# Two cross-attention layers written as one straight program, with the last slot of layer 1 joined to the first of layer 2

## What is computed

```python
res = x
h = _layer_norm(x, ln1_scale, ln1_offset)
x = res + _cross_attention(h, xf_1, wq1, bq1, wk1, bk1, wv1, bv1, wo1, bo1, bias_k1, bias_v1)
res = x
h = _layer_norm(x, ln2_scale, ln2_offset)
x = res + _cross_attention(h, xf_2, wq2, bq2, wk2, bk2, wv2, bv2, wo2, bo2, bias_k2, bias_v2)
```

## Time and profile before

| | |
|---|---|
| time, median of 3 runs | 1511.86 us (1509.45 to 1514.3) |
| profiled execution, first to last instruction (span) | 1511.0 us |
| mean granted PE clock | 0.966 of full speed |
| first slot starts | 34.39 us |
| layer 2 starts (its front-only slot) | 547.49 us |
| first matmul behind the two layers | 1063.45 us |

### The profile page before, as it was taken

The page is one execution under the profiler, slowest core; times in us unless marked ns, Lnnn a source line. Parts: engine busy times, 40 slices in busy tenths (PEclk is TensorE's granted clock), DMA queues, the critical chain, the costliest instruction groups (busy, mean ns, idle before and its releaser), DMA issues. The chain is left out here.

```text
span 1511.0 us, 29462 instructions
## 1 busy us (share of the span) xinstructions
PE 1426.2 (94%) x11575; PEld 1274.8 (84%) x11575; DVE 895.5 (59%) x1929; ACT 626.1 (41%) x1053; POOL 340.7 (23%) x322
## 2 busy tenths in 40 slices
PE   4999999999999899999999999998898999997898
PEld 3899899899998778988998999986787888887787
DVE  6566567566666646666665666665523377776422
ACT  4533344334333543433343344343422336666521
POOL 4201101101011111101101011020754035555654
PEclk8999999999999979999999999997899999999899
DMA  5000000000000000000000000000000000001000
GB/s 169 29 29 1 30 5 25 30 1 29 29 2 29 1 30 1 29 29 1 29 1 30 29 1 29 29 1 1 25 0 8 0 1 1 0 0 60 4 28 28
DMA packets 28991, 30.42 MB, mean 20 GB/s; under 512 B 651, under 2 KB 28883, under 8 KB 28883
## 3 DMA queue, kind: packets, MB, share of 16 engines
q1 hardware_dynamic: 28658, 28.72, 6.0%
q10 hardware_dynamic: 226, 0.10, 0.0%
HBM read 26.72 MB, written 2.10 MB: 19 GB/s over the span
## 5 line engine op out<-in xcount | busy, mean ns | idle before, releaser
L296 POOL TENSOR_TENSOR WLO<-W,WHI 128x512 fp32r<-128x512 f32 x68 | 85.1, 1283 | 793.5 <-DVE WHI L623 793.5
L168 PE MATMUL bank<-SRC_HI,WHI 128*128 128x512 f32 (+1 forms) x576 | 233.4, 405 | 18.5 <-issue 14.6
L169 PE MATMUL bank<-SRC_LO,WHI 128*128 128x512 f32 (+1 forms) x576 | 231.9, 403 | 0.0
L170 PE MATMUL bank<-SRC_HI,WLO 128*128 128x512 f32 (+1 forms) x576 | 231.5, 402 | 0.0
L570 DVE STREAM_TRANSPOSE PRT<-PR 32x256 f32<-32x256 f32 x512 | 223.3, 436 | 8.4
L591 DVE TENSOR_TENSOR CLO<-bank,CHI 128x512 fp32r<-128x512 f32 x128 | 88.2, 691 | 159.3 <-ACT CHI L502 159.1
L478 ACT ACTIVATE QT<-bank,PB 128x512 f32<-128x512 f32 x128 | 88.2, 690 | 209.2 <-PE bank L170 209.2
L168 PE MATMUL bank<-WHI,CHI 128*128 128x256 f32 x512 | 155.2, 303 | 0.0
L168 PE MATMUL bank<-WHI,SRC_HI 128*128 128x256 f32 x512 | 149.4, 292 | 0.0
L168 PEld LDWEIGHTS bank<-SRC_HI,WHI 128*128 128x128 f32 x576 | 111.2, 193 | 42.7 <-issue 15.4
L170 PE MATMUL bank<-WHI,CLO 128*128 128x256 f32 x512 | 145.6, 284 | 0.0
(11 more groups left out here) (182 smaller groups left out, 2976.5 us busy)
## 6 DMA issues: line engine op xcount, KB each, us to landing
W<-in_wall SPq DMA_DIRECT2D x18, 1024.0 KB, 5.6
V<-in_ctx SPq DMA_DIRECT2D x4, 512.0 KB, 5.5
X<-in_x SPq DMA_DIRECT2D x4, 512.0 KB, 6.5
mlp_w<-in_w SPq DMA_DIRECT2D x2, 1024.0 KB, 7.4
out<-X SPq DMA_DIRECT2D x4, 512.0 KB, 3.0
W<-in_qw SPq DMA_DIRECT2D x1, 256.0 KB, 3.9
W<-in_kw SPq DMA_DIRECT2D x1, 256.0 KB, 4.1
W<-in_vw SPq DMA_DIRECT2D x1, 256.0 KB, 4.9
```

The source lines that it names most:

```text
L168: e.matmul(dst, a_hi, b_hi, start=start, stop=False, **kw)
L169: e.matmul(dst, a_hi, b_lo, start=False, stop=False, **kw)
L170: return e.matmul(dst, a_lo, b_hi, start=False, stop=stop, **kw)
L296: i = e.tensor_tensor(WLO[a][:, j, :, :], W[a][:, j, :, :], WHI[a][:, j, :, :].bitcast(F32), ALU.subtract)
```

## The change

The hardware loops are gone: each engine's program is written out for 65 slots, numbered n = 0 to 64 over both layers. A new class works out what a slot has to do. Slot 32 has the back of layer 1's last unit and the front of layer 2's first. The norm's group 3 moves from the slot that was `at` 0 to the slot behind it: n = 1 for layer 1, n = 33 for layer 2. Waits and addresses become constants. In the bridge slots the PE program is otherwise as before.

```diff
+            class Slot:
+                def __init__(self, n):
+                    self.n, self.front, self.back = n, n < NL * UNITS, n > 0
+                    self.L, self.pair, self.g = n // UNITS, n // G, n % G
+                    self.a, self.ab = self.pair % 2, (n - 1) // G % 2
+                    self.Lb, self.hp, self.gb = (n - 1) // UNITS, (n - 1) // G % HP, (n - 1) % G
+                    self.bridge = self.back and self.hp == HP - 1
+                    self.nk, self.ng = (n + 2) // UNITS, (n + 2) % UNITS
+                    self.norm = self.back and self.ng < G
+                    self.parts = self.Lb * G + self.gb + 1
+            def slots(e, slot, begin=None):
+                for n in range(NL * UNITS + 1):
+                    if begin is not None and n % UNITS == 0 and n < NL * UNITS:
+                        begin(e, n // UNITS)
+                    slot(Slot(n))
...
 # SP
-                    with e.Fori(1, SETS // 2) as i:
-                        for a in range(2):
+                    for m in range(2, SETS):
...
 # POOL
-                    with e.Fori(0, NL) as L:
+                    for L in range(NL):
                         norm_lo(e, norm, L, G - 1)
-                        split(L * HP + 1, 1)
-                        with e.Fori(0, HP // 2 - 1) as i:
-                            for a in range(2):
-                                split(L * HP + i * 2 + 2 + a, a)
-                        split(L * HP + HP, 0)
+                        for m in range(L * HP + 1, L * HP + HP + 1):
+                            split(m, m % 2)
...
 # PE: before the key projection
-                                if j == 1 and norm_now is not None:
-                                    e.wait_ge(norm.scaled, (norm_now[0] * G + norm_now[1]) * DC)
-                                if j == 1 and at == 1:
-                                    e.wait_ge(norm.scaled, (L + 1) * G * DC)
+                                if j == 1:
+                                    if n == 0:
+                                        e.wait_ge(norm.scaled, (G - 1) * DC)
+                                    elif before.norm:
+                                        e.wait_ge(norm.scaled, (before.nk * G + before.ng + 1) * DC)
...
-                        if at == 0:
-                            e.wait_ge(k_out, 2 * n + 2)
-                            norm_turn(e, norm, *norm_now, PROJ[2:])
...
-                        if norm_now is not None and bridge and front:
-                            e.wait_ge(ptb_out, L * G + at - LASTP)
-                            norm_turn(e, norm, *norm_now, PROJ[2:])
+                        if s.norm and front:
+                            if s.bridge:
+                                e.wait_ge(ptb_out, s.parts)
+                                e.wait_ge(bw_out, s.Lb + 1)
+                            norm_turn(e, norm, s.nk, s.ng, PROJ[2:])
...
 # PE and ACT
-                    with e.Fori(0, NL) as L:
-                        slots(e, L, slot)
+                    slots(e, slot)
...
 # DVE
-                    with e.Fori(0, NL) as L:
+                    def begin(e, L):
                         e.memset(BWT[:, :, :], 0.0).then_inc(bwt_sum, 1)
                         e.wait_ge(bwt_sum, L * BWTN + 1)
-                        e.tensor_copy(BWT[:, :, H + 1], PM[:, bass.ds(L * LNP + 4, 2)]).then_inc(bwt_sum, 1)
-                        slots(e, L, slot)
+                        e.tensor_copy(BWT[:, :, H + 1], PM[:, L * LNP + 4:L * LNP + 6]).then_inc(bwt_sum, 1)
+                    slots(e, slot, begin)
```

More of the change, by code:

```diff
@@ L317, in _, with slot @@
                 def _(e):
[L318 to L320 removed]
+                    def slot(s):
+                        n, g, a, front, back = s.n, s.g, s.a, s.front, s.back
                         toks = slice(g * GTOK, (g + 1) * GTOK)
[L322 removed]
                         if front:
                             if g == 0:
[L326 to L329 removed]
+                                e.wait_ge(w_split, s.pair + 1)
+                            if n % UNITS < G:
+                                e.wait_ge(norm.lo, (s.L * G + g + 1) * DC)
+                            before = Slot(n - 1)
                             for j, half, done, free in ((0, 1, q_done, v_out), (1, 0, k_done, k_out)):
[L331 to L339 removed]
+                                if j == 1:
[3 more added lines that the diff above has]
+                                        e.wait_ge(norm.scaled, (before.nk * G + before.ng + 1) * DC)
+                                    if n > 0 and before.bridge:
+                                        e.wait_ge(ptb_out, before.parts)
+                                        e.wait_ge(bw_out, before.Lb + 1)
                                 for h in range(2):
@@ L430, in slot @@
                                     dst = bank[3 + j][:, p * 256:(p + 1) * 256]
-                                    if bridge:
-                                        e.matmul(dst, PTT[:, (at - LASTP - 1) % 2, ts], BW[:, :], start=True, stop=False)
+                                    if s.bridge:
+                                        e.matmul(dst, PTT[:, s.gb % 2, ts], BW[:, :], start=True, stop=False)
                                     for h in range(2):
-                                        i = three(e, dst, CHI[:, h, ts], CLO[:, h, ts], WHI[ab][:, 3, h, :],
-                                                  WLO[ab][:, 3, h, :], h == 0 and not bridge, h == 1)
+                                        i = three(e, dst, CHI[:, h, ts], CLO[:, h, ts], WHI[s.ab][:, 3, h, :],
+                                                  WLO[s.ab][:, 3, h, :], h == 0 and not s.bridge, h == 1)
                                 i.then_inc(o_done, 1)
-                        if norm_now is not None and not front:
-                            norm_turn(e, norm, *norm_now, PROJ[2:])
+                        if s.norm and not front:
+                            norm_turn(e, norm, s.nk, s.ng, PROJ[2:])
                     e.wait_ge(ident_done, 1)
@@ L465, in _, with slot @@
                     e.wait_ge(ctx_lo, G * DC)
-                    with e.Fori(0, NL) as L:
-                        slots(e, L, slot)
+                    slots(e, slot)
                 @block.scalar
                 def _(e):
[L471 to L474, removed]
+                    def slot(s):
+                        n, a, front, back = s.n, s.a, s.front, s.back
                         if front:
@@ L485, in values_out @@
                             e.wait_ge(v_done, 2 * n + j + 1)
-                            e.activation(V[at % 2][:, 2 * j:2 * j + 2, :],
+                            e.activation(V[n % 2][:, 2 * j:2 * j + 2, :],
                                          PROJ[j][:, :].rearrange("p (t n) -> p t n", n=256),
                                          ACT.Copy).then_inc(v_out, 1)
-                        if at == 0:
-                            norm_sqrt(e, norm, *norm_now)
                         if front:
                             values_out(0)
[L494 to L498, removed]
+                        if s.bridge:
+                            e.wait_ge(ptb_turned, s.parts)
+                            e.activation(PTT[:, s.gb % 2, :], PROJ[2][0:32, :], ACT.Copy).then_inc(ptb_out, 1)
+                        if s.norm and front:
+                            norm_sqrt(e, norm, s.nk, s.ng)
                         if back:
@@ L502, in slot @@
                                 e.activation(CHI[:, h, :], bank[3 + h][:, :], ACT.Copy).then_inc(c_hi, 1)
[L503 to L504 removed]
+                        if s.norm and not front:
+                            norm_sqrt(e, norm, s.nk, s.ng)
                         if front:
                             values_out(1)
[L507 to L511, removed]
                             e.wait_ge(sub_done, n + 1)
                             e.activation(ex[:, :, :], sub[:, :, :], ACT.Exp, scale=SCALE).then_inc(exp_done, 1)
[L514 to L517 removed]
+                        if s.norm:
+                            e.wait_ge(cur_set, s.nk + 1)
+                            norm_scale(e, norm, s.nk, s.ng, PROJ[2:])
                     e.dma_start(vh, vech.rearrange("(a r) k -> r a k", a=2)).then_inc(vec_in, 16)
@@ L543, in _, with slot @@
                     logit = logits[:, :, 0:GT * KEYS].rearrange("p h (t k) -> p h t k", k=KEYS)
[L545 to L548, removed]
+                    def slot(s):
+                        n, g, a, gb, hp, front, back = s.n, s.g, s.a, s.gb, s.hp, s.front, s.back
                         if front:
                             if g == 0:
-                                e.wait_ge(w_split, pair + 1)
+                                e.wait_ge(w_split, s.pair + 1)
                             e.tensor_copy(KT[:, :, :, S], PB[a][:, 2, :].unsqueeze(2).to_broadcast([P, 2, GTOK // S])
@@ L572, in slot @@
                             i.then_inc(pt_out, 1)
```

(22 more changed lines are left out.)

50 lines of the change are left out of this document (14 added, 36 removed).

## The result

The changed kernel takes 1476.11 us (median of four runs, 1474.2 to 1477.0); the kernel before took 1513.08 us beside it (median of four, 1509.45 to 1514.56). The ratio is 0.9755, 95% interval 0.9739 to 0.977. The forecast was 1475.2 us. The profiled execution of after took 1476.23 us, its span 1474.5 us where before's was 1511.0 us: 36.5 us to account for.

The account below looks back on a forecast made before the run. PE, busy 94% of the span, was taken as the bound, with time to win only where it stands still or at half clock. 1511.0 − 22.7 − 15.1 + 1.2 = 1474.4, so median 1475.2 us; range 1467 to 1486 us.

Parts of the forecast that it names:

- The jumps: PE's four jumps back in the slot loop go: 22.7 us gained, 14.6 us of it gaps, the rest lost clock.
- The upper of the two bounds: Gain from removing PE's four jumps back: 22.7 us if the clock recovers too, against 14.6 us for the gaps alone.
- Rival (c): PE's four gaps belong to their place in the work, not to the jump, and stay: 1498 us; chance 0.02.
- The joined slot: Layer boundary: slots 31 to 33 take 55.1 us in place of 70.17 us, 15.1 us gained.
- The lower bound of this gain: Layer boundary gains only 10.9 us if slot 33's wait grows to a jump's gap and costs 5.4 us.
- The start: Slots 0 and 1 of layer 1: norm group 3 moves into slot 1 and PE waits for CLO, 1.2 us lost.
- Costed at nothing: Constants for registers, SP's and POOL's loops as lists, straight code on all engines: no time gained or lost.
- rival (d): Constants in place of registers speed PE's waits, 0.1 us for each slot, 6.4 us in all: 1469 us; chance 0.05.
- rival (b): Loading straight code holds up DVE and ACT, 16 times, costing 57 us: 1532 us; chance 0.07.
- up to 1 us: Slot 34's key projection waits for ACT's norm copies: costed at nothing, this much if slot 33's cover is short.
- Rival (a): Norm in slots 1 and 33 makes PE's CLO wait 3.65 us and the clock fall: 1484 us; chance 0.10.
- The sum: Whole kernel: 1511.0 − 22.7 − 15.1 + 1.2 = 1474.4 us, with 0.86 us added for the median 1475.2 us.

Follow-up runs that it names:

- Experiment 1: The kernel before with PE's program alone written out straight, other engines still looping, layers not joined: 1488.62 us, ratio 0.9844.
- experiment 4: The changed kernel with slots 9 to 24 of each layer looped on PE alone, two passes over eight slots: 1486.48 us, ratio 0.9841.
- experiment 5: The changed kernel with four short PE loops over one already met wait, at slots 9, 17, 41 and 49: 1476.49 us, ratio 0.9771.
- experiment 2: The kernel before with every engine but PE written out straight, PE keeping both loops, layers not joined: 1512.72 us, ratio 1.0004.

## Why the prediction was right

**The jumps.** Forecast 22.7 us, of which 14.6 are gaps. From the windows, slots 3 to 30 gave 11.89 us and slots 34 to 62 gave 10.33 + 0.57 for the longer slot 34, 22.8 in all. The upper of the two bounds was right: the clock's loss went with the gaps. Experiment 1 puts it on PE's program alone, 4 on the jumps, 5 on jumps over that much code. Rival (c), gaps that belong to the place, fell with the windows, in which the same work at the same four places has no gap, and for good with experiment 4, in which slot 17 of each layer has its gap back behind a jump and slot 9 has none.

**The joined slot.** Forecast 55.1 us as 18.9 + 19.7 + 16.5; measured 54.95 as 18.91, 19.73 and 16.30. The bridge slots came out of before's windows as they stood. Slot 33's wait was forecast at 1.1 us and took 0.84: ended by CLO, as said, and the term that was off is DVE's chain: PE wanted CLO 12.54 us after the slot's start (forecast 12.5), and DVE had it at 13.33 (forecast 13.6). With slot 34's 0.57 the boundary gave 14.65 us for 15.1. The lower bound of this gain, written as 10.9 us, is 10.8 by its own terms, 16.2 − 5.4; nothing hangs on it.

**The start.** Forecast +1.2 us, measured +1.36 in slots 0 and 1, and mostly not for the reason given. CLO's wait in slot 1 is there, 0.75 us, but the wait for softmax, which was to stay at 0.9 us, fell to 0.53. So PE stands still for 1.28 us (29.35 − 28.07) where it was 0.90 (27.99 − 27.09), 0.38 us more. The other 0.98 us is PE's busy time, at clock 0.94 for 0.96. The first matmul at full speed (0.39 us) starts 3.9 us into slot 0, where before it was 2.2 us. The prediction did not have this, and why the clock rises later there is open. So the size of this term came out right by luck.

**Costed at nothing.** Constants sped up nothing: a pair takes 29.55 us for the 29.54 worked out from loop code, and rival (d) fell. Straight code for DVE and ACT cost nothing either; experiment 2 took rival (b) by itself, and found 1.0004; in after neither DVE nor ACT has a wait for "issue" between 60 and 1000 us. The Trainium skill, "Runtime: NRT & Kernel Launch", section Instruction fetch mechanics, by which the crossing into the next block is mostly hidden, agrees with that. What did not hold is the slot behind the norm. It takes 0.57 us more in both layers, 1.1 us in all, and by another mechanism than the one for which "up to 1 us" was named there: not late copies of the norm on ACT, but POOL's norm remainder, of which the prediction had said only that its order stays.

**Rival (a)** needed a wait of 3.65 us before CLO; the waits are 0.84 and 0.75 us, and the clock stays at 1.00 at the boundary.

**The sum.** Against before's span it was 36.6 us, and the span lost 36.5. That these agree to 0.1 us is in part luck: what was not forecast is 1.1 us lost in slots 2 and 34, and 1.0 us gained outside the slots. The prediction also took the profiled execution's time for its span and added 0.86 us for the median. But a run's time is longer than its span: 1476.23 us for 1474.5 in after's profiled execution, and 1.7 to 1.8 us in every run that has both on record. That makes up most of the 0.9 us by which 1476.11 misses 1475.2.

## What to carry to other kernels

Find a loop's price where the bounding engine stands still behind a long branch, in a window from slot to slot: it holds the gap and, where it came, the clock's fall behind it. Here writing out that one engine's program won both, while the others' loops could have stayed. The stage that drained the pipeline between two loops cost more here than the loop's jump, and was mended by giving it the next stage's work. When work is moved into a slot, look also one slot further, at what the other engines run then: here POOL's remainder met DVE's small operations there.

## What was not expected of the hardware

**The price of a jump on PE** differs with what it goes back to. Over eight slots it took 5.15 to 5.82 us, in three kernels; over one instruction at most 0.234 us; and the MLP's loop of after, whose body takes 23 us, is cheap too. Its line:

```profile
L657 PEldq COMPARE_BRANCH  x6: 76/210/238, 1069.2 to 1462.7; - x6
```

Not taken, a branch took 0.074 to 0.083 us. The amount of code is not all of it: the layer loop's jump, over more code than the slot loop's, took 3.43 us in before and 3.30 in experiment 2. While the ten slot-loop jumps ran, a weight set of 1 MB was being loaded, and at these two none was. The load alone makes no gap, since after has the same loads at the same places; whether it lengthens a jump was not tested. The Trainium skill, "Runtime: NRT & Kernel Launch", section Instruction fetch mechanics, says that a taken branch to code outside the window that is loaded must fetch it first; the runs agree with that, though no row shows such a fetch holding PE. The Trainium skill, "Advanced Engine Details and Errata", section Control Flow Timing, has one figure for a compare-and-branch, about 108 ns, and the rows differ from it in both directions. At what amount of code the step comes was not tried.

**The clock does not fall behind every such gap.** Gaps of 3.42 us (experiment 2, the pair at 786.08: 33.22 − 29.80) and 3.53 us (experiment 4, at 759.49) left it at 1.00, and those pairs lost 3.7 and 3.8 us in all; the slot behind each is an ordinary one at 1.00 too. Gaps of 3.40 us (150.35) and 3.38 us (266.91) took it to 0.90 and 0.91, and cost 6.4 and 6.5 us. Length alone doesn't tell them apart; what does stays open, and with it some 2.7 us for each jump.

**A small DVE operation can stand still for as long as one of POOL's runs.** DVE's copy of 16 elements a partition took 1.05 us for 0.18, and its product of 8 elements 0.48 us for 0.17, each to the end of a POOL subtraction; the reduction and the reciprocal between them kept their 0.68 and 0.20 us. The Trainium skill, "SBUF — State Buffer", section SBUF: two separate sides, says that DVE and GpSimd share a pair of ports that one of them holds for a whole instruction, which DVE wants for its 2-port modes and, against a GpSimd operation that reads SBUF, for two inputs in SBUF. The trace agrees for the product, which has two inputs, and for the reduction and the reciprocal, which have one; that the copy runs in such a mode no run here shows. What such a meeting costs is not fixed: in experiment 5 DVE's next product in slot 2, of 512 elements, took 1.85 us for 0.68 behind the two held ones, and PE waited 1.43 us for the value product there.
